# A layer of routed experts: rows sorted by expert into tiles of 128 slots

## The reference

```
def _moe_forward(x, gate_w, w_gate_up, w_down, shared_w_gate_up, shared_w_down):
    # HIDDEN 512, 16 experts of MOE_INTER 128, TOP_K 2, SHARED_INTER 512
    gu_s = x2 @ shared_w_gate_up.T
    g_s, u_s = jnp.split(gu_s, 2, axis=-1)
    shared_out = jax.nn.silu(g_s) * u_s @ shared_w_down.T
    logits = x2 @ gate_w.T
    probs = jax.nn.softmax(logits, axis=-1)
    topk_vals, topk_idx = jax.lax.top_k(probs, TOP_K)
    topk_vals = topk_vals / jnp.sum(topk_vals, axis=-1, keepdims=True)
    combine = jnp.sum(jax.nn.one_hot(topk_idx, NUM_EXPERTS, dtype=x2.dtype) * topk_vals[..., None], axis=1)
    gu = jnp.einsum('th,eih->eti', x2, w_gate_up)
    g, u = jnp.split(gu, 2, axis=-1)
    act = jax.nn.silu(g) * u
    out_e = jnp.einsum('eti,ehi->eth', act, w_down)
    moe_out = jnp.einsum('eth,te->th', out_e, combine)
    return (moe_out + shared_out).reshape(orig_shape)
```

## Time and profile before

| | before |
|---|---|
| median of 3 runs | 3311.49 us |
| the profiled execution | 3311.82 us, of which the span of its trace is 3309.9 |
| mean granted clock of TensorE | 0.978 |
| busy in the span | PE 3189.8 us (96%), DVE 2156.1 (65%), ACT 1690.3 (51%), POOL 870.1 (26%) |
| the routed-experts stage | PE's first expert matmul at 2950.35 us, end of the span at 3309.9 |

### The profile page before, as it was taken

One profiled execution on the slowest core, in us unless ns is written; L12 is line 12 of the kernel. 1 busy time (PEld: TensorE's weight loads), 2 busy tenths in 40 slices (PEclk: granted clock), 3 DMA queues, 4 the chain that ended last, 5 costly groups with the idle time before them and its releaser, 6 DMA issues. The chain is left out here.

```text
span 3309.9 us, 55163 instructions
## 1 busy us (share of the span) xinstructions
PE 3189.8 (96%) x18912; PEld 2819.3 (85%) x18912; DVE 2156.1 (65%) x3234; ACT 1690.3 (51%) x3173; POOL 870.1 (26%) x703
## 2 busy tenths in 40 slices
PE   8999998999999999999999999899898999989999
PEld 8888886999999998999989999787678888868887
DVE  4333333888888887888878888544555667745555
ACT  4343343776667666676666766422424444432222
POOL 0000121444444443444434444322002223400000
PEclk9999998999999999999999999899897999989999
DMA  7665785777667776767767775475202001111111
GB/s 249 216 214 190 239 271 173 155 164 161 161 159 158 162 163 154 159 159 160 163 154 158 160 162 130 142 244 178 87 1 68 28 27 40 40 39 48 48 38 45
DMA packets 360310, 452.26 MB, mean 137 GB/s; under 512 B 32316, under 2 KB 289644, under 8 KB 360072
## 3 DMA queue, kind: packets, MB, share of 16 engines
q1 hardware_dynamic: 360072, 449.22, 51.2%
HBM read 201.45 MB, written 113.43 MB: 95 GB/s over the span
## 5 line engine op out<-in xcount | busy, mean ns | idle before, releaser
L724 POOL TENSOR_TENSOR a_t_lo<-a_turned,a_t_hi 128x512 fp32r<-128x512 f32 x512 | 648.9, 1288 | 941.1 <-ACT a_t_hi L853 941.1
L844 ACT ACTIVATE a_probs<-a_ps_s,a_neg_max 128x1024 f32<-128x1024 f32 (+1 forms) x512 | 529.1, 1034 | 476.0 <-DVE a_neg_max L896 470.4
L889 DVE TENSOR_REDUCE a_half_max<-a_ps_s 128x1 f32<-128x1024 f32 (+1 forms) x512 | 571.0, 1115 | 192.5 <-PE a_ps_s L741 188.3
L739 PE MATMUL a_ps_s<-a_k_buf,a_q_buf 128*128 128x512 f32 (+1 forms) x1024 | 419.8, 410 | 17.6 <-ACT a_probs L844 11.7
L740 PE MATMUL a_ps_s<-a_k_buf,a_q_buf 128*128 128x512 f32 (+1 forms) x1024 | 386.1, 377 | 0.0
L741 PE MATMUL a_ps_s<-a_k_buf,a_q_buf 128*128 128x512 f32 (+1 forms) x1024 | 385.9, 377 | 0.0
L925 DVE TENSOR_TENSOR a_x_lo<-a_ps_x,a_x_hi 128x512 fp32r<-128x512 f32 (+1 forms) x512 | 314.3, 614 | 107.6 <-ACT a_x_hi L862 107.6
L915 DVE STREAM_TRANSPOSE a_turned<-xn 128x512 f32<-128x512 f32 x512 | 357.4, 698 | 0.0
L471 DVE TENSOR_TENSOR p_out<-p_ps_j,p_out 128x512 fp32r<-128x512 f32 (+3 forms) x196 | 153.0, 781 | 304.4 <-ACT p_out L399 304.4
L739 PE MATMUL a_ps_o<-a_t_hi,a_v_buf 128*128 128x256 f32 x1024 | 299.2, 292 | 5.6 <-issue 3.1
L399 ACT ACTIVATE p_out<-p_ps_j 128x512 fp32r<-128x512 f32 (+3 forms) x196 | 142.0, 725 | 313.3 <-PE p_ps_j L292 313.3
(11 more groups left out here) (319 smaller groups left out, 7378.6 us busy)
## 6 DMA issues: line engine op xcount, KB each, us to landing
xn<-a_probs SPq DMA_DIRECT2D x1024, 128.0 KB, 3.4
a_q_all<-p_out SPq DMA_DIRECT2D x64, 512.0 KB
a_q_buf<-a_q_all SPq DMA_DIRECT2D x128, 256.0 KB, 3.2
a_k_buf<-a_k_all SPq DMA_DIRECT2D x64, 464.5 KB, 4.0
a_v_all<-p_out SPq DMA_DIRECT2D x56, 512.0 KB
a_k_all<-p_out SPq DMA_DIRECT2D x48, 384.0 KB
a_v_buf<-a_v_all SPq DMA_DIRECT2D x64, 256.0 KB
a_o_all<-a_o_part SPq DMA_DIRECT2D x128, 128.0 KB, 3.1
```

What stands on the lines that cost most here:

```text
L724: pool.tensor_tensor(t_lo[:, slot, :, :], turned[:, slot, :, :], t_hi[:, slot, :, :].bitcast(F32), ALU.subtract).then_inc(t_done, 1)
L739: pe.matmul(o, w_hi, m_hi, start=first, stop=False)
L844: act.activation(probs[j][u.a][:, lo:hi], s_flat[:, lo:hi], ACT.Exp, bias=neg_max[:, j:j + 1], scale=SCALE, accum_out=half_sum[:, bass.ds( ...
L889: dve.reduce_max(half_max[:, half:half + 1], s_flat[:, lo:hi], AX.X).then_inc(max_done, 1)
```

## The change

The routed experts no longer run over all tokens. Each token has two choices, so there are 2048 rows of (token, choice). They are placed by expert into tiles of 128 slots, each tile holding rows of one expert; with 16 experts, 2 x 1024 / 128 + 16 - 1 = 31 tiles always suffice, and 31 are always computed, with unused slots zero.

Where a row goes is worked out after the top two: DVE adds up the chosen masks (`mask`, and `earlier`, running sums over the token tiles), PE multiplies them with a triangle and with ones for each row's rank in its expert and for the totals (`rank`, `totals`), and DVE makes from these the number of tiles of each expert (`counts`), their ends and starts, the slot of each row (`slot_of`, in two halves, one for each choice) and the expert of each tile (`expert_id`).

The rows lie in DRAM: `x_slots` for the inputs of the experts, `y_slots` for their results. POOL fills 2 MB of a buffer (`picked[1]`) with zeros, SP writes `x_slots` with it in 4 transfers, then POOL issues 16 indirect transfers (one for each token tile and choice) that scatter the rows of `xn` to their slots.

For each tile SP reads the expert's number into a register (`value_load`), loads that expert's weights (512 and 256 KB) and the tile's 128 rows (256 KB) into one of three raw buffers, and stores the result of the tile five before (256 KB). PE transposes the rows (part 0), the weights (parts 1, 2 and 3) and the activations (`routed_turn`), and does 12 up matmuls of 256 columns and 3 down matmuls of 512. ACT has per tile four high parts of 128x512, a Silu and a high part of 128x128 and a copy of the result into `g_y`; DVE four low parts, a product and a low part of 128x128. Part 3 writes the down weights with a step of four elements, as the transposes leave them.

Three pieces of the shared expert stand in front of the tiles, with an addition without weight, and the fourth behind them. After the last store of `y_slots`, POOL issues 16 indirect transfers that gather, for each token, its two result rows into `picked`; ACT scales the first by its weight, DVE adds the second by its own (`mix`), adds the sum to `x_res`, and the tiles are stored as before.

The core of the diff:

```diff
+            if part == 3:
+                return (by_chunk(ps_t[:, part % 2, :]), gd_hi[a][:, :].rearrange("p (q c) -> p c q", c=DC),
+                        gd_lo[a][:, :].rearrange("p (q c) -> p c q", c=DC))
...
+            def load_expert(i):
+                a = i % RAW
+                if i >= RAW:
+                    sp.wait_ge(g_t_ps, PARTS * (i - RAW + 1))
+                e = sp.value_load(expert_id[0:1, i:i + 1], min_val=0, max_val=E - 1)
+                sp.dma_start(g_up[a][:, :, :], w_gate_up[bass.ds(e, 1), :, :].rearrange("a (k p) h -> p (a k) h", p=P)
+                             ).then_inc(g_w_loaded[a], 16)
+                sp.dma_start(g_down[a][:, :, :], w_down[bass.ds(e, 1), :, :].rearrange("a (p c) i -> p (a c) i", p=P)
+                             ).then_inc(g_w_loaded[a], 16)
+            def load_tokens(i):
+                sp.dma_start(g_x[i % RAW][:, :], x_slots[P * i:P * (i + 1), :]).then_inc(g_x_loaded[i % RAW], 16)
+            def store_tokens(i):
+                sp.wait_ge(gy_copied, i + 1)
+                sp.dma_start(y_slots[P * i:P * (i + 1), :], g_y[i % 2][:, :]).then_inc(gy_stored[i % 2], 16)
...
+            for s in range(2):
+                load_shared(s)
+            sp.wait_ge(zeros_set, 1)
+            for n in range(0, NT, TILES):
+                m = min(TILES, NT - n)
+                sp.dma_start(x_slots[P * n:P * (n + m), :].rearrange("(n p) d -> p n d", p=P), picked[1][:, 0:m, :]).then_inc(cleared, 16)
+            for s in range(2, SHARED):
+                load_shared(s)
+            sp.wait_ge(experts_done, 1)
+            for i in range(RAW):
+                load_expert(i)
+            sp.wait_ge(scattered, 16 * CHOICES * TILES)
+            for i in range(RAW):
+                load_tokens(i)
+            for i in range(RAW, NT):
+                load_expert(i)
+                load_tokens(i)
+                if i >= 5:
+                    store_tokens(i - 5)
+            for i in range(NT - 5, NT):
+                store_tokens(i)
...
+            pool.memset(picked[1][:, :, :], 0.0).then_inc(zeros_set, 1)
...
+            pool.wait_ge(slots_done, 1)
+            pool.wait_ge(cleared, 16 * -(-NT // TILES))
+            for t in range(TILES):
+                for k in range(CHOICES):
+                    pool.indirect_dma_start(x_slots, bass.IndirectOffsetOnAxis(ap=slot_of[:, k, t:t + 1], axis=0),
+                                            xn[:, t, :], None).then_inc(scattered, 16)
+            pool.wait_ge(scattered, 16 * CHOICES * TILES)
+            for a in range(2):
+                pool.wait_ge(gy_stored[a], 16 * ((NT - a + 1) // 2))
+            for t in range(TILES):
+                for k in range(CHOICES):
+                    pool.indirect_dma_start(picked[k][:, t, :], None, y_slots,
+                                            bass.IndirectOffsetOnAxis(ap=slot_of[:, k, t:t + 1], axis=0)).then_inc(picked_loaded[t], 16)
...
+            def routed_transpose(i, part):
+                a, q = i % RAW, PARTS * i + part
+                if part == 0:
+                    pe.wait_ge(g_x_loaded[a], 16 * (i // RAW + 1))
+                if part == 1:
+                    pe.wait_ge(g_w_loaded[a], 32 * (i // RAW + 1))
+                if q >= 2:
+                    pe.wait_ge(g_done, q - 1)
...
+            for quarter in range(4):
+                up(0, 0, quarter)
+            pe.wait_ge(pads_set, 6)
+            pe.wait_ge(masks_done, 1)
+            pe.matmul(rank, before[:, :], mask[:, :, :], start=True, stop=False)
+            pe.matmul(rank, ones[:, :], earlier[:, 0:TILES, :], start=False, stop=True)
+            pe.matmul(totals, ones[:, :], earlier[:, TILES, :], start=True, stop=True).then_inc(rank_ps, 1)
...
+            pe.wait_ge(slots_done, 1)
+            down(0, 0)
+            transpose_weights(1, 2)
+            down(0, 1)
+            shared(1, follows=True)
+            shared(2, follows=True, following=False)
+            down(2, 2)
+            routed_transpose(0, 0)
+            down(2, 3)
+            routed_transpose(0, 1)
...
+            for i in range(NT):
+                last = i == NT - 1
+                if last:
+                    pe.wait_ge(g_done, PARTS * NT)
+                    transpose_weights(3, 0)
+                else:
+                    routed_transpose(i + 1, 0)
+                routed_up(i, 0)
+                if i:
+                    routed_turn(i - 1)
+                if last:
+                    transpose_weights(3, 1)
+                else:
+                    routed_transpose(i + 1, 1)
+                routed_up(i, 1)
+                if not last:
+                    routed_transpose(i + 1, 2)
+                if i:
+                    routed_down(i - 1)
+                if last:
+                    transpose_weights(3, 2)
+                else:
+                    routed_transpose(i + 1, 3)
+            pe.wait_ge(g_act_done, NT)
+            shared(3, routed_tail=True, following=False)
+            pe.wait_ge(gy_copied, NT)
             for t in range(2, TILES):
-                down(N - 1, None, 1, t)
+                down(3, t)
...
+            def routed_copy(i):
+                a = i % 2
+                act.wait_ge(gy_ps, i + 1)
+                if i >= 2:
+                    act.wait_ge(gy_stored[a], 16 * (i // 2))
+                act.activation(g_y[a][:, :], ps_y[:, a, :], ACT.Copy).then_inc(gy_copied, 1)
...
+            for t in range(TILES):
+                act.wait_ge(picked_loaded[t], 32)
+                act.activation(picked[0][:, t, :], picked[0][:, t, :], ACT.Copy, scale=best[:, t:t + 1]).then_inc(weighed, 1)
...
+            dve.wait_ge(rank_ps, 1)
+            chain.link(dve.tensor_tensor(over[:, :, :], wide(totals, TILES), steps[:, :].unsqueeze(1).to_broadcast([P, E, TILES]), ALU.is_gt))
...
+            for k, one_hot in enumerate((first, second)):
+                chain.link(dve.tensor_tensor(hit[:, :, :], one_hot[:, :, :], slots[:, :, :], ALU.mult))
+                chain.link(dve.reduce_sum(row[:, :], hit[:, :, :], AX.X))
...
+            def mix(t):
+                dve.wait_ge(weighed, t + 1)
+                chain.link(dve.scalar_tensor_tensor(picked[1][:, t, :], picked[1][:, t, :], runner[:, t:t + 1], picked[0][:, t, :],
+                                                    ALU.mult, ALU.add))
 
             for t in range(TILES):
                 dve.wait_ge(xt_hi_done, t + 1)
@@ -2233,31 +2467,118 @@
             dve.tensor_tensor(gate_lo[:, :, :], ps_h[:, 0, 0, 0:DC * E].rearrange("p (c e) -> p c e", c=DC),
                               gate_hi[:, :, :].bitcast(F32), ALU.subtract).then_inc(gate_done, 1)
             for job in range(JOBS):
-                weights_lo(0, 0, job)
+                weights_lo(0, job)
             dve.wait_ge(logits_ps, 1)
             dve.tensor_copy(logits[:, :, :], ps_y[:, 0, 0:TILES * E].rearrange("p (t e) -> p t e", t=TILES)).then_inc(logits_out, 1)
             dve.wait_ge(logits_out, 1)
             softmax_rows(dve, chain, scores[:, :, :], logits[:, :, :], row[:, :], row2[:, :], exp_done, centred)
-            dve.wait_ge(pads_set, 2)
+            dve.wait_ge(pads_set, 6)
             top_two(dve, chain, scores[:, :, :], ramp[:, :], hit[:, :, :], first[:, :, :], second[:, :, :], rest[:, :, :],
                     row[:, :], best[:, :], runner[:, :])
+            chain.link(dve.tensor_tensor(mask[:, :, :], first[:, :, :], second[:, :, :], ALU.add))
+            for t in range(TILES - 1):
+                chain.link(dve.tensor_tensor(earlier[:, t + 1, :], earlier[:, t, :], mask[:, t, :], ALU.add))
+            dve.tensor_tensor(earlier[:, TILES, :], earlier[:, TILES - 1, :], mask[:, TILES - 1, :], ALU.add).then_inc(masks_done, 1)
             chain.link(dve.tensor_tensor(row[:, :], best[:, :], runner[:, :], ALU.add))
             chain.link(dve.reciprocal(row[:, :], row[:, :]))
             chain.link(dve.tensor_tensor(best[:, :], best[:, :], row[:, :], ALU.mult))
             chain.link(dve.tensor_tensor(runner[:, :], runner[:, :], row[:, :], ALU.mult))
-            chain.link(dve.tensor_tensor(first[:, :, :], first[:, :, :], wide(best[:, :], E), ALU.mult))
-            chain.link(dve.tensor_tensor(second[:, :, :], second[:, :, :], wide(runner[:, :], E), ALU.mult))
-            chain.link(dve.tensor_tensor(share[:, :, 0:E], first[:, :, :], second[:, :, :], ALU.add))
-            expert(None, 0, 0)
-            with dve.Fori(0, N // 2 - 1) as i:
-                expert(2 * i, 2 * i + 1, 1)
-                expert(2 * i + 1, 2 * i + 2, 0)
-            expert(N - 2, N - 1, 1, following=False)
-            product(N - 1, 1)
-            add(N - 1, None, 2)
-            product_lo(N - 1, 1)
+            dve.wait_ge(rank_ps, 1)
+            chain.link(dve.tensor_tensor(over[:, :, :], wide(totals, TILES), steps[:, :].unsqueeze(1).to_broadcast([P, E, TILES]), ALU.is_gt))
```

(105 more changed lines are left out.)

335 lines of the change are left out of this document (217 added, 118 removed).

## The result

The changed kernel takes 3221.54 us, the median of four runs (3219.8 to 3226.03); against the kernel before the ratio is 0.9728 [0.9711, 0.9745], some 90 us less. The forecast was 3188, in a range of 3163 to 3265. So the time lies in the range and on the right side, but over a quarter of the gain that was forecast (some 123 us) did not come. The profiled execution took 3226.03, with a span of 3224.3.

A forecast was written before the change was run, and what follows sets the result against it. PE's own work was taken to bound the stage of 20 experts. Tiles start at 3009.5, 31 tiles add 140.4 and the tail 35.3, ending at 3185.2 in the span; forecast 3188 us, range 3163 to 3265.

The forecast's parts named there:

- What bounds the tile: Routed tiles: PE's work is 4.1 us, but waiting for DVE to free a transpose bank makes 4.53, 31 tiles 140 us.
- the write of part 3: Down weights written with a step of four: taken at ACT 0.60 and DVE 0.69 us, as without a step.
- the sign of 4.5 us between the first transposes of tiles: Expected in the profile after: PE's first transposes of successive tiles about 4.5 us apart.
- Twice would add 1.3 us: If part 3's stepped write took twice as long, the other bank would make the tile 5.8 us, +40 us overall.
- The tail: From the tiles' end at 3149.9 through 16 gathers at 1.3 us to the program's end: 35.3 us.
- lie inside: After the tiles: the shared expert behind them, 16.3 us of PE matmuls, would be hidden within the 35.3 us tail.
- The sign that PE would be idle in the last 15 us: Expected in the profile after: 16 gathers behind one another, with PE idle in the last 15 us.
- The front: Router and three shared experts before the tiles: 48.9 matmuls, 4.5 transposes, 4.6 router, 1.1 wait; tiles start at 3009.5.
- A: Rival: slow indirect transfers, 3.4 us each, make the first tile 16 us late and the tail 32 longer: 3236; 18%.
- B: Rival: SP or the transfers pace the tiles, at 5.3 us a tile, +24 us: 3212; 17%.
- C: Rival: TensorE's clock stays at 1.2 GHz in the tiles, 8.0 us a tile, 109 us later: 3297; 9%.
- D: Rival: transfers in the tiles run no faster than 154 to 164 GB/s; 8.7 us a tile, 3318, slower; 4%.

The follow-up runs named there:

- e4_noload: Changed kernel with expert weights loaded for the first three tiles only, later tiles computing with those; 3221.16 us, 0.9734 of the kernel before.
- e5_banks: Changed kernel with a PSUM bank for each of the four parts instead of two in turn, stepped write kept; 3199.92 us, 0.9668 of the kernel before.
- e6_read: Changed kernel with part 3's step moved from the SBUF write to the PSUM read; 3193.09 us, 0.9648 of the kernel before.
- e3_tail: Changed kernel with the last shared piece's second half ahead of the gathered rows on ACT and DVE; 3214.02 us, 0.9711 of the kernel before.
- e11_read_tail: Changed kernel with part 3's step on the read and the last shared piece's second half ahead of the gathered rows; 3192.15 us, 0.9652 of the kernel before.
- e7_rows_banks: Changed kernel with down weights loaded in 512-byte rows so part 3 needs no step, and four banks; 3185.67 us, 0.9623 of the kernel before.
- e10_read_banks_behind: Changed kernel with part 3's step on the read, four banks, two shared pieces behind the tiles, ACT's and DVE's order there new; 3177.58 us.

## Why the prediction was right, and where it was off

**What bounds the tile: right in kind, mis-sized in one term.** In the tiles PE waits for the bank, and neither for SP nor for the transfers, and its own work (4.1) doesn't fill them; e4_noload and e5_banks show it. The step that failed is the write of part 3, of which the prediction said "Lower bound the same 0.60 and 0.69, upper bound twice that; I take the same, since the width is the same". It measured 1.085 and 1.084, 1.8 and 1.6 times, the bank of part 3 became the slower one, and the 31 tiles took 24.7 us more; the sign of 4.5 us between the first transposes of tiles failed with it. Without the step the tile is 4.55 against 4.53 forecast.

"Twice would add 1.3 us" doesn't follow from the prediction's own prices: part 3's bank would be 3.30, PE's work from part 1 to part 3 is 0.45 + 0.71 + 0.45 + 0.68 = 2.29, and the tile 5.59, not 5.8. With the two measured operations the same sum is 2.89 + 2.29 = 5.18; of the rest to 5.36, 0.1 is the way from DVE back to PE, 0.15 us in the rows above where 0.05 was taken. The range held the result because its upper end, unlike the forecast, had priced a slower write.

The Trainium skill, "Vector Engine (DVE) Microarchitecture Reference", section 5.2 on measured stream behaviour, says that an SBUF port streams at its full rate only while elements come in adjacent pairs. For a column it has 1.054 ns without a step, 1.71 where the destination alone jumps 4 KiB at each element, and 2.50 where it steps by 24 words. An estimate from these rows is 0.34 to 0.74 us more for 512 columns; the trace has 1.084 - 0.692 = 0.39, inside that, with a step of four words, for which the page has no row, and with the same step in a source. e6_read shows that reading PSUM with a step cost nothing here. That page speaks against the value that I took, and I had not weighed it.

**The tail: one wait was missed.** Sixteen gathers, 1.3 us each and 8.6 us behind the last tile: right. But the prediction let the shared piece behind "lie inside" without following ACT's order, in which its second half stands behind the fifth scaling: 6.0 us by e3_tail. The sign that PE would be idle in the last 15 us failed too: its last down products run from 3207.72 to 3213.1. The other 2.6 are what e3_tail has left over the forecast, nearly all at its last gather: 4.82 us to its landing instead of 2.6, and a scaling of 0.73 instead of 0.6.

**The front.** The router cost PE 2.23 us of waiting, 0.66 of small matmuls and 1.57 of waiting, 4.5 in front of the first down product, where 4.6 were forecast. Of the 2.2 us over, 0.8 are PE's waits among the first transposes of tile 0 (0.53 and 0.24) and 0.6 its wait for the last addition, 1.69 instead of 1.1; 0.8 is left open.

**The rivals.** A, B, C and D did not come: 1.25 us for each gather, SP waiting 90.6 us, clock 1.00, and 229 to 259 GB/s in windows of 20 us in the tiles of the changed kernel, with 304 to 309 where more was asked. That the time came out near A and B (3236 and 3212) is chance. With both faults mended (e11_read_tail) the stage is 263.2 against 256.8 forecast. Of these 6.4, 3.0 are the front (84.1 instead of 81.1), 2.6 the first gather to the end (29.3 instead of 26.7), and 0.9 the tiles and their end. The front was not followed further.

## What to carry to other kernels

Where two PSUM banks are handed round between three engines, add up each bank's whole cycle and not the engines' work: a step in one part's writes, 0.9 us on two engines that were idle for a quarter of the time and more, became PE's wait tile after tile. Where a step is needed, try it on both sides; here it cost nothing on the side that reads PSUM. When work is said to lie inside a wait, follow each engine's order through that wait: an instruction behind a wait for data is as late as the data.

## What the runs showed of the hardware

- A write of 128x512 float32 to SBUF with a step of four elements (16 bytes): ACT 1.085 us instead of 0.60, DVE 1.084 instead of 0.69 (DVE reads one source from SBUF with the same step). The same values read from PSUM with a step of 128 elements and written without one: 0.59 and 0.69.
- An indirect transfer of 128 rows of 2 KB: POOL is mostly busy for 0.95 us and starts one every 1.25 to 1.3; a gather lands 3.3 to 3.8 us after its issue in the changed kernel. The six gathers of e3_tail that run beside the stores of the result start 1.38 to 1.61 us apart and land after 4.7 to 5.2.
- Reading one expert number into a register of SP: 0.27 us, about 0.5 with the register operations behind it.
- Matmuls of 512 columns: 0.23 us apart at a granted clock of 1.00, 0.43 apart at 0.52, behind a wait of PE of 12.21 us.
- 304 to 309 GB/s of loads and stores with PE busy for 97 to 98.6% (e7_rows_banks and e10_read_banks_behind); in e7_rows_banks PE waited for them 0.9 us in 118.
